# Attention value products before the weighing instead of behind it, and banks emptied in halves by two engines

## The reference

```python
def mha(xq, ctx, wq, wk, wv, wo, bo):
    ...
    scores = jnp.einsum('bhqd,bhkd->bhqk', q, k) / math.sqrt(DH)
    attn = jax.nn.softmax(scores, axis=-1)
    out = jnp.einsum('bhqk,bhkd->bhqd', attn, v)
    out = out.transpose(0, 2, 1, 3).reshape(b, sq, INNER)
    return out @ wo + bo

h1 = adaln(x, t, norm1_w, norm1_b)
x = mha(h1, h1, attn1_wq, attn1_wk, attn1_wv, attn1_wo, attn1_bo) + x
h2 = adaln(x, t, norm2_w, norm2_b)
x = mha(h2, context, attn2_wq, attn2_wk, attn2_wv, attn2_wo, attn2_bo) + x
h3 = adaln(x, t, norm3_w, norm3_b)
x = glu_ff(h3, ff_w1, ff_b1, ff_w2, ff_b2) + x
```

## Time and profile before

| | us |
|---|---|
| median of 3 runs | 2136.75 |
| lowest, highest run | 2133.06, 2137.06 |
| span of the profiled execution | 2124.9 |
| PE busy | 2039.6 |
| DVE busy | 1323.4 |
| ACT busy | 1386.2 |
| POOL busy | 1071.9 |

### The profile page before, as it was taken

One profiled execution on the slowest core, in us unless ns is written; L12 is line 12 of the kernel. 1 busy time (PEld: TensorE's weight loads), 2 busy tenths in 40 slices (PEclk: granted clock), 3 DMA queues, 4 the chain that ended last, 5 costly groups with the idle time before them and its releaser, 6 DMA issues. The chain is left out here.

```text
span 2124.9 us, 38735 instructions
## 1 busy us (share of the span) xinstructions
PE 2039.6 (96%) x11068; PEld 1337.7 (63%) x11068; DVE 1323.4 (62%) x3389; ACT 1386.2 (65%) x2659; POOL 1071.9 (50%) x1198
## 2 busy tenths in 40 slices
PE   7899999999999999999999999999999889899996
PEld 5455555555555555555555565555555558799996
DVE  5554657676767676767676666666656545455565
ACT  4566666676667676767676767676766666566663
POOL 2444444636363637363737373737363445556664
PEclk9999999999999999999999999999999999999998
DMA  4110111121111111111111111111122312222256
GB/s 153 45 26 25 50 35 51 46 50 45 49 45 50 46 53 45 49 45 49 45 49 45 49 45 51 47 48 52 44 54 64 96 48 57 58 56 72 60 185 215
DMA packets 136321, 127.35 MB, mean 60 GB/s; under 512 B 14665, under 2 KB 110569, under 8 KB 136234
## 3 DMA queue, kind: packets, MB, share of 16 engines
q1 hardware_dynamic: 127466, 109.11, 18.7%
q0 software_dynamic: 8768, 17.20, 2.5%
HBM read 86.63 MB, written 40.67 MB: 60 GB/s over the span
## 5 line engine op out<-in xcount | busy, mean ns | idle before, releaser
L1928 POOL TENSOR_TENSOR pr<-pr,sm 128x512 f32<-128x512 f32 x256 | 277.7, 1098 | 483.7 <-DVE sm L1462 483.7
L1126 ACT ACTIVATE kp<-ps 128x512 f32<-128x512 f32 x512 | 298.9, 601 | 179.5 <-PE ps L283 176.2
L834 PE MATMUL ps<-tt,V 128*128 128x512 f32 x768 | 380.3, 593 | 3.5 <-ACT tt L1126 3.5
L1452 DVE TENSOR_REDUCE mx<-ps 128x8 f32<-128x512 f32 x256 | 176.8, 691 | 306.3 <-PE ps L783 306.3
L1126 ACT ACTIVATE tt<-ps 128x512 f32<-128x512 f32 x512 | 275.2, 591 | 40.2 <-PE ps L813 39.6
L783 PE MATMUL ps<-kp,hf 128*64 128x256 f32 x2048 | 276.8, 392 | 6.9 <-DVE pr L1455 3.9
L283 PE MATMUL ps<-cT,M 128*128 128x512 f32 x768 | 262.0, 464 | 0.0
L783 PEld LDWEIGHTS ps<-kp,hf 128*64 128x64 f32 x2048 | 124.4, 136 | 196.9 <-DVE pr L1455 142.4
L1126 ACT ACTIVATE pt<-ps 128x512 f32<-128x512 f32 x256 | 153.6, 600 | 141.4 <-PE ps L795 139.1
L283 PE MATMUL ps<-hk,M 128*128 128x512 f32 x768 | 242.2, 438 | 0.0
L941 PE MATMUL ps<-xT,wt 128*128 128x128 f32 (+1 forms) x1728 | 221.9, 278 | 4.0 <-DVE wt L1753 4.0
(11 more groups left out here) (235 smaller groups left out, 3470.3 us busy)
## 6 DMA issues: line engine op xcount, KB each, us to landing
mod<-emb_s SPq DMA_DIRECT2D x96, 256.0 KB, 4.3
xr<-rows_s SPq DMA_DIRECT2D x144, 66.0 KB
cb<-y_s SPq DMA_DIRECT2D x32, 256.0 KB
x_in<-in_x_dram SPq DMA_DIRECT2D x16, 256.0 KB, 4.4
xn_s<-x_in SPq DMA_DIRECT2D x16, 256.0 KB, 2.1
res<-xn_s SPq DMA_DIRECT2D x16, 256.0 KB, 2.8
c_in<-in_ctx_dram SPq DMA_DIRECT2D x16, 256.0 KB, 4.7
y_s<-res SPq DMA_DIRECT2D x16, 256.0 KB, 2.0
```

The costliest lines, as they stand in the source:

```text
L834: mm = nc.tensor.matmul(psO[:], Vw[a][:, g * HG + head_at(h), :], tt[:, h, :], start=(g == 0 and h == 0), stop=ends)
L1126: return nc.scalar.activation(o, i, ACT.Copy)
L1452: nc.vector.tensor_reduce(mx[:, p % 2, :], heads(psS[p % 2][:]), AX_X, ALU.max).then_inc(max_done, 1)
L1928: tensor(v, v, sm[:, p, :].unsqueeze(2).broadcast_to([P, HG, 64]), ALU.mult).then_inc(prob_done, 1)
```

## The change

- The value products come first. For each tile of 128 tokens and each half of the unit's heads, `values` multiplies the split `hk` or `cT` (as stationary operand) by the split V of four heads: three fp32r matmuls of 512 columns. That is 8 products in a unit, and they stand in the slot of their own unit, behind the weighing of the unit before and ahead of the keys of the next one. V is split in the setup, whole.
- A value bank holds two sequences. ScalarE copies its partitions 0 to 63 (`values_hi`), VectorE its partitions 64 to 127 (`values_odd`) to the new tile `vp`, in which two heads lie over one another on 128 partitions. Value products go round the ring together with the keys.
- `weigh` is now transposed probabilities times `vp`: per tile p four pairs of heads m and two sequences s, 8 fp32 matmuls of 128 columns with a stationary operand of 128 x 64, straight into `psO`. `project`, `split`, `last_split`, `last_rest`, `out_attn` and both turns back go. `psO` has tokens on its partitions, and VectorE adds it to the residual in two tiles of their own, `y1r` and `y2r`, to which GpSimd adds the bias (`add_bias`). `after_attn1` moves from slot 3 to slot 2, `after_attn2` from slot 1 to slot 0.
- `scores` has two matmuls of 512 columns, one for each sequence, in place of four of 256.
- The order in the slot: four T one after the other in three banks, then scores 0, and from there scores p+1 ahead of weigh p. `RINGS` has 6, 6, 4 and 3 banks, now for 16 products; the GLU's second half has a bank of its own, `psF`.
- VectorE's odd copies stand between and behind `total` 2 and 3 and ahead of all hooks of the slot; ScalarE does all exponentials, then all even copies, then the keys.

The core of the diff:

```diff
-        psS, psM, psT, psO = psum[0:2], psum[2], psum[4], psum[7]
-        pstw = [psum[5:7], psum[2:4]]
-        psH = psum[3]
-
-        RINGS = ([*psum[5:7], psT, psH, *psS], [*psum[5:7], psT, psH, *psS], [*psum[5:7], psT, psH], [*psum[5:7], psH])
...
+        psS, psM, psT, psF, psO = psum[0:2], psum[2], psum[3:6], psum[6], psum[7]
+
+        RINGS = ([psS[0], *psT, psF, psS[1]], [psS[0], *psT, psF, psS[1]], [psF, *psT], [psT[2], psT[0], psT[1]])
+        FIRST_KEYS = [psum[5], psum[6], psum[3]]
...
+        def products(i, u):
+
+            return ([("v", s) for s in range(2 * NT)] if live(i, u) else []) + ([("k", h) for h in range(HG)] if live(*after(i, u)) else [])
+
+        def bank_of(i, u, kind, x):
+
+            return RINGS[u][products(i, u).index((kind, x)) % len(RINGS[u])]
+
+        def emptied(i, u, kind, x):
+
+            return [(vp_even, v_count(i, u, x)), (vp_odd, v_count(i, u, x))] if kind == "v" else [(kp_done, k_count(*after(i, u), x))]
+
+        def left_in(i, u, bank):
+
+            made = [at for at in products(i, u) if bank_of(i, u, *at) is bank]
+            return emptied(i, u, *made[-1]) if made else []
...
+            def values(i, u, s, bank):
+
+                a, g = divmod(u, 2)
+                t, e = divmod(s, 2)
+                heads = slice(HG * g + HH * e, HG * g + HH * e + HH)
+                src = hk if a == 0 else cT
+                mm3(bank[:], lambda k: src[:, k, t * P:(t + 1) * P],
+                    lambda k: Vw[a][:, k, heads, :].rearrange("p h d -> p (h d)")).then_inc(v_done, 1)
...
-                    for j in range(2):
-                        mm = nc.tensor.matmul(psS[p % 2][64 * j:64 * j + 64, :].rearrange("p (h s k) -> p h s k", h=HH, s=2)[:, :, s, :],
-                                              hf[u // 2][:, cols], kp[:, j * HH:(j + 1) * HH, cols], start=True, stop=True)
-                        if s == 1:
-                            mm.then_inc(s_done, 1)
+                    mm = nc.tensor.matmul(psS[p % 2][64 * s:64 * s + 64, :].rearrange("p (h k) -> p h k", h=HG),
+                                          hf[u // 2][:, cols], kp[:, :, cols], start=True, stop=True)
+                mm.then_inc(s_done, 1)
...
-                if not (isinstance(n, int) and n < 1):
-                    pe.wait_ge(pt_done, n)
+                for w in left_in(i, u, psT[p]) if p < 3 else [(pt_done, n - 2)]:
+                    wait(w)
                 pe.wait_ge(prob_done, n + 1)
                 for k in range(4):
-                    mm = nc.tensor.transpose(psT[:, k * P:(k + 1) * P], pr[:, p, k * P:(k + 1) * P], ident[:])
+                    mm = nc.tensor.transpose(psT[p % 3][:, k * P:(k + 1) * P], pr[:, p, k * P:(k + 1) * P], ident[:])
                 mm.then_inc(T_done, 1)
...
-                if p >= 2:
-                    for w in t_free(i, u, p - 2):
-                        wait(w)
-                pst = pstw[p % 2]
-                for s in range(2):
-                    rows = slice(64 * s, 64 * s + 64)
-                    nc.tensor.matmul(pst[s][:], tm[rows, p, :], pt[rows, p % 2, :], start=True, stop=True).then_inc(t_done, 1)
-
-            def project(i, u, h):
-
-                a, g = divmod(u, 2)
-                if h == 0:
-                    pe.wait_ge(tt_done, t_count(i, u, 3))
-                if h == 0 and g == 0:
-
-                    if a == 0 and ok(i - 2):
-                        pe.wait_ge(o_out[1], i - 1)
-                    if a == 1:
-                        pe.wait_ge(o_out[0], i + 1 if ok(i) else NC)
-                ends = g == 1 and h == HG - 1
-                if u in RU and h >= HF:
-                    if h == HF:
-                        pe.wait_ge(tr_lo, 3 * split_seq(i, u) + 3)
-                        pe.wait_ge(last_lo, split_seq(i, u) + 1)
-                    halves = tt_h[:, h - HF, :], tt_l[:, h - HF, :]
-                    mm = mm3(psO[:], lambda k: Vr[u][:, k, h - HF, :], lambda k: halves[k], first=False, last=ends)
-                else:
-                    mm = nc.tensor.matmul(psO[:], Vw[a][:, g * HG + head_at(h), :], tt[:, h, :], start=(g == 0 and h == 0), stop=ends)
-                if h == HG - 1:
-                    mm.then_inc(o_done, 1)
+                pe.wait_ge(vp_even, v_count(i, u, 2 * p + 1))
+                pe.wait_ge(vp_odd, v_count(i, u, 2 * p + 1))
+                for m in range(4):
+                    for s in range(2):
+                        mm = nc.tensor.matmul(psO[64 * s:64 * s + 64, p * D:(p + 1) * D], pt[:, p, m * P + 64 * s:m * P + 64 * s + 64],
+                                              vp[:, 2 * p + s, m * D:(m + 1) * D], start=(g == 0 and p == 0 and m == 0), stop=(g == 1 and p == NT - 1 and m == 3))
+                if g == 1 and p == NT - 1:
+                    mm.then_inc(o_done[a], 1)
...
+                if last:
+                    for p in range(NT):
+                        turn(li, lu, p)
+                if u == 0 and ok(i - 3) and not c_last(i - 3):
+                    glu_down(i - 3, FT - 1)
+                if here:
+                    if u == 3 and ok(i - 2):
+                        pe.wait_ge(glu, FT * (i - 2) + 1)
+                    if u == 0 and ok(i - 3):
+                        pe.wait_ge(glu, FT * (i - 2))
+                    scores(i, u, 0)
...
                 for p in range(NT):
+                    if here and p < NT - 1:
+                        scores(i, u, p + 1)
...
+                        weigh(li, lu, p)
+
+                def product(kind, x):
+                    made, banks = products(i, u), RINGS[u]
+                    j = made.index((kind, x))
+                    bank = banks[j % len(banks)]
+                    if j >= len(banks):
+                        for w in emptied(i, u, *made[j - len(banks)]):
+                            wait(w)
+                    elif bank in psT and last:
+                        pe.wait_ge(pt_done, 4 * seq(li, lu) + (4, 2, 3)[psT.index(bank)])
+                    elif bank in psS and here:
+                        pe.wait_ge(sub_done, 4 * seq(i, u) + 3 + psS.index(bank))
+                    elif bank in psS and isinstance(i, int) and i == NC:
+                        pe.wait_ge(eu_act, 3 * E)
+                    elif bank is psF and u < 2 and ok(i - 3):
+                        pe.wait_ge(f2_out, i - 2)
+                    if kind == "v":
+                        values(i, u, x, bank)
+                    else:
+                        keys(*after(i, u), x, bank)
+
+                if here:
+                    for s in range(2 * NT):
+                        product("v", s)
...
+                act.wait_ge(T_done, 4 * seq(i, u) + p + 1)
+                copy(pt[:, p, :], psT[p % 3][:]).then_inc(pt_done, 1)
+
+            def values_hi(i, u, s):
+                t, rows_to = half_of(s)
+                act.wait_ge(v_done, v_count(i, u, s))
+                copy(vp[rows_to, 2 * t, :], bank_of(i, u, "v", s)[0:64, :]).then_inc(vp_even, 1)
...
+                if last:
+                    for p in range(NT):
                         turn_hi(li, lu, p)
-                    if u == 0 and p == 0 and ok(i - 3):
-                        out_glu(i - 3)
-                    if p >= 1 and here:
-                        exp(i, u, p - 1)
-                    if p >= 1 and last:
-                        weigh_hi(li, lu, p - 1)
-                if last:
-                    weigh_hi(li, lu, 3)
+                if u == 0 and ok(i - 3):
+                    out_glu(i - 3)
                 if here:
-                    exp(i, u, 3)
-                hooks = {0: ((1, 0, tm_split), (3, 1, lambda c: ln_hi(c, 1)), (5, 1, context)),
+                    for p in range(NT):
+                        exp(i, u, p)
+                    for s in range(2 * NT):
+                        values_hi(i, u, s)
...
+            def values_odd(i, u, s):
+                t, rows_to = half_of(s)
+                dve.wait_ge(v_done, v_count(i, u, s))
+                nc.vector.tensor_copy(vp[rows_to, 2 * t + 1, :], bank_of(i, u, "v", s)[64:128, :]).then_inc(vp_odd, 1)
...
-                dve.wait_ge(back1, c + 1)
-                dve.wait_ge(ld_xn, 16 * c + 16)
-                tensor(res[:], tiles3(psT[:]), res[:], ALU.add).then_inc(y1_done, 1)
+                dve.wait_ge(o_done[0], c + 1)
+                dve.wait_ge(bias_done[0], c + 1)
+                tensor(y1r[:], tiles3(psO[:]), y1r[:], ALU.add).then_inc(y1_done, 1)
...
+                if here:
+                    total(i, u, 2)
+                    values_odd(i, u, 0)
+                    total(i, u, 3)
+                    for s in range(1, 2 * NT):
+                        values_odd(i, u, s)
...
+            def add_bias(c, a):
+
+                if first(c):
+                    pool.wait_ge(ld_b, 64)
+                pool.wait_ge(ld_y1 if a else ld_xn, 16 * c + 16)
+                row = y2r if a else y1r
```

(1 more changed line is left out.)

376 lines of the change are left out of this document (102 added, 274 removed).

## The result

The changed kernel takes 2171.1 us (median of 4 runs, 2167.1 to 2172.7) where the kernel before took 2135.3 on the same chip: 1.0168 times as long, with an interval of 1.0152 to 1.0185. It is slower by 36 us. The forecast was 2081, with a range of 2020 to 2145, so both the sign and the range were missed. The nearest rival was C, 2175 to 2200.

The account below looks back on a forecast made before the run. TensorE was taken as the bound: 104.8 - 5.0 - 6.2 = 93.6 us per round, 100.9 with waits. Twelve rounds x -3.9 = -47, start and drain -10, setup +1 gave 2081 us, 80% range 2020 to 2145.

Parts of the forecast that it names:

- Rival C: VectorE becomes the bound: a round 107.7 to 109.7 us, +3 to +5, total 2175 to 2200; chance 0.12.
- PE's prices: TensorE's group times without waiting: T 1.95, S 0.86, W 0.89, products 0.70 us; a round 93.6 instead of 104.8.
- Rival D: Weighing pairs do not overlap: W at 1.78 us, +14 per round less what waits hide, over 2250; chance 0.04.
- E: S and W keep a gap at each change, seven of 0.15 us per unit: +2 per round, 2108; chance 0.12.
- F: PE's sequencer limits the weighing to one instruction each 108 ns: +3 us per round, 2120; chance 0.04.
- VectorE's load: VectorE's busy time per round, with the odd copies added: from 69.0 to 89.7 us.
- Peaks, totals and odd copies slide by 1 to 2 us: Slot 2: late VectorE and GpSimd chains delay this work; with other waits +4.1 us, slot 26.6.
- 2.4 us of the products' ring: Slot 2: PE's wait in the value products with a ring of four banks, 2.4 us.
- ring of three: Slot 3: second odd copy holds the fifth product, +1.05 us; `glu_up` waits, +0.55; slot 28.7.
- Outside the rounds: Start and drain units -10 us (0 to -25), setup +1 us (0 to +4).

Follow-up runs that it names:

- e_early: Changed kernel with ln1's statistics and roots moved to slot 0 and GpSimd's y1r bias put ahead of ln3's root: ratio 0.9918 to the kernel before.
- e_bias: Changed kernel with only GpSimd's y1r bias moved ahead of ln3's root: ratio 1.0090 to the kernel before.
- e_turns: Changed kernel with slot 2's ring reordered, first GELU ahead of key copy 4, ln1's input copies behind slot 3's second probability copy: ratio 0.9977 to the kernel before.
- e_gate: Changed kernel with ScalarE's small gate exponential moved from slot 3 to the start of slot 0, gates and first scatters following: ratio 1.0090 to the kernel before.
- e_odd: Changed kernel with all eight of VectorE's odd copies ahead of totals 2 and 3: ratio 1.0105 to the kernel before.
- c_five: c_three with odd copies ahead of totals 2 and 3 in slot 3 only, and GpSimd's ln4 root ahead of ln1's in slot 0: ratio 0.9750 to the kernel before.
- c_three: Changed kernel with the moves of e_early, e_turns and e_gate together: ratio 0.9718 to the kernel before.
- c_four: c_three with the odd copies ahead of totals 2 and 3 in all slots: ratio 0.9987 to the kernel before.

## Why the prediction failed, step by step

- **PE's prices: right.** S and W at 0.88 each, T of 16 at 1.91, products at 0.70; slots 0 and 1 came within 0.2 and 0.5 of the forecast. Rival D (weighing pairs one after the other), E (gaps between S and W) and F (the sequencer: 32 instructions of W follow in 1.84 us, 57 ns each) did not come. VectorE's load was right too: 88.4 us a round, 89.7 forecast.
- **Slot 2, "Peaks, totals and odd copies slide by 1 to 2 us": mis-sized, 3.0.** I had the chain (norm3, ln1's statistics, GpSimd) and let it end 3.7 us into the slot. It ended at 5.95: `stats3` 0.9 later, `norm3` 2.06 instead of 1.12 since the new bias runs beside it, and a shorter slot 1. The contention I had read for the statistics in rows 8 I did not apply to an operation whose new neighbour the change itself puts there. And I counted the delay only as 2.4 us of the products' ring; the third S's own wait of 2.9 was missing. e_early and e_bias show both parts.
- **Slot 3, "ring of three": a step was missing.** T is ahead of everything else in the slot and writes the banks of the last keys of slot 2. That wait, 2.1 us in slot 3 and 0.5 at the end of slot 2, stands in no term; e_turns takes 1.5 off slot 3 and 0.7 off slot 2. The products' wait was 1.7 for 1.05, the GLU's some 2.2 (14.4 us from the first key to the end for 12.2 of matmuls) for 0.55; I had named the order on VectorE, but not ScalarE's two loads of the table between GELUs, which the projections had covered (e_gate).
- **Outside the rounds: wrong sign.** -9 forecast. The two traces have +13, the medians less the rounds only +5 (36 - 31), since the profiled execution of before was a fast one; the 11.85 us that I put outside its span are mostly that. Clear of this is the setup: the first T comes 7 us later, where I had +1. No run looked into it, and its cause stays open.
- **Rival C** said when the kernel gets slower: over 15.1 us of a round with VectorE idle. It was 19.2 (107.6 - 88.4), within the 18 to 20 held possible, and 2171 lies just under its 2175. Its chance of 0.12 was too small. But its sentence "VectorE becomes the bound" holds only in part: in slot 2 the load stayed and the time went away (e_early), and in slot 3 VectorE's row is the bound up to the GLU only once the odd copies stand ahead of the totals (e_odd, c_five). The waits of T and most of the GLU's were for ScalarE (e_turns, e_gate). So the range of C was nearly met for another reason than the one that it gave.
- **c_three is luck, not a late hit.** Its round of 100.5 is next to the 100.9 of the forecast, but with moves that the forecast did not have, and its slots 29.7, 23.8, 22.1 and 24.9 are not the forecast's 28.7, 23.1, 22.5 and 26.6.

## What to carry to other kernels

When a change takes the slack from the engine that bounds, list for each slot what the bounding engine does first, and follow back who empties the banks it writes; a wait there counts in full, and removing a later wait gives nothing if the same engine's row ends in the next one. Cost each new operation of GpSimd at the VectorE operations that will run beside it. Move chains ahead of their slot before judging a faster order of matmuls: the same instructions were 1.7% slower than before in one order and 2.8% faster in another.

## What the runs showed of the hardware

- TensorE's granted clock fell to its lower level (0.50 to 0.52 in windows of 3.05 to 3.5 us) in rounds that were otherwise full, and the length of one wait does not tell when. It fell behind the third S's wait of 2.74 us in six of ten rounds of the changed kernel, but behind the same wait in none of eleven rounds of e_gate; behind the waits of 2.04 in slots 1 and 2 of c_four in all of eleven; behind 1.83 in two of twelve in e_odd; and in four of eleven rounds of e_bias behind two waits of 0.97 and 0.61. Where nothing else was waited for behind it, a fall cost 1.5 us more than the wait itself (e_bias, 28.6 and 30.1).
- The copy of half a bank, 64 partitions of 512, costs ScalarE 591 ns and VectorE 694, as much as a whole one (594 for a key bank).
- GpSimd beside it made VectorE's four `norm3` instructions take 2.06 instead of 1.12 us. The page "GPSIMD Engine Reference", section "1. Specifications", of the Trainium skill has the two engines share their ports to SBUF for some forms of VectorE's instructions; the trace agrees in that the statistics of 0.86 us (L1345) did not slow.
